# Carrying three dense streams through all stages, and writing a product's bias with one matmul

## The reference

```
h = relu(layernorm(x)); x = x + gcn(h, edges)
h = relu(layernorm(x)); x = x + sage(h, edges)      # two convolutions with W_l, W_r, b
h = relu(layernorm(x)); x = x + mlp_gnn(h, edges)   # messages by a 2-layer MLP, update by one, layernorm, gamma, beta
h = relu(layernorm(x)); x = x + mean_gnn(h, edges)  # W_self, W_neighbor, bias
```

## Time and profile before

| | |
|---|---|
| median of 3 runs | 6238.43 us |
| profiled execution, span | 6243.6 us |
| PE busy | 4227.3 us, 68% |
| DVE busy | 4147.6 us, 66% |
| ACT busy | 3656.1 us, 59% |
| POOL busy (inside DMA instructions) | 3838.7 us, 61% |
| mean granted PE clock | 0.836 |

### The profile page before, as it was taken

One profiled execution on the slowest core, in us unless ns is written; L12 is line 12 of the kernel. 1 busy time (PEld: TensorE's weight loads), 2 busy tenths in 40 slices (PEclk: granted clock), 3 DMA queues, 4 the chain that ended last, 5 costly groups with the idle time before them and its releaser, 6 DMA issues. The chain is left out here.

```text
span 6243.6 us, 88780 instructions
## 1 busy us (share of the span) xinstructions
PE 4227.3 (68%) x25124; PEld 3337.9 (53%) x25124; DVE 4147.6 (66%) x20553; ACT 3656.1 (59%) x9152; POOL 3838.7 (61%) x3228
## 2 busy tenths in 40 slices
PE   1173777777566766998958888886888846545444
PEld 1052555556455555777736666664666634434333
DVE  1094777778699995776747777785999945434334
ACT  0003767767577774776746677774877845434333
POOL 6605666675577765776747677765777654544554
PEclk7596888888788887999979999998999967667666
DMA  9903656666466664666658788884555531211221
GB/s 251 311 2 112 181 154 172 167 166 169 115 153 151 148 144 113 146 144 132 130 147 220 209 225 216 225 204 113 136 132 128 122 77 58 76 53 63 66 65 36
DMA packets 891523, 878.84 MB, mean 141 GB/s; under 512 B 131106, under 2 KB 671660, under 8 KB 890962
## 3 DMA queue, kind: packets, MB, share of 16 engines
q1 hardware_dynamic: 546568, 575.48, 29.0%
q0 software_dynamic: 224000, 235.91, 22.7%
q10 hardware_dynamic: 120460, 61.78, 3.7%
HBM read 345.70 MB, written 533.16 MB: 141 GB/s over the span
## 5 line engine op out<-in xcount | busy, mean ns | idle before, releaser
L2061 POOL DMA_INDIRECT out<-final_y,leads x200 | 202.2, 1011 | 434.8 <-DVE final_y L2188 328.8
L1151 POOL DMA_INDIRECT node<-gcn_comb,leads x200 | 325.2, 1626 | 193.0 <-ACT gcn_comb L1176 92.5
L1151 POOL DMA_INDIRECT sums<-mean_comb,leads x200 | 327.6, 1638 | 154.1 <-ACT mean_comb L1176 84.4
L1151 POOL DMA_INDIRECT node<-sage_comb,leadh x200 | 329.4, 1647 | 142.4 <-DMA node<-sage_comb,leadh 60.8
L444 PE MATMUL final_p<-wT,final_hT 128*128 128x128 f32 x800 | 223.0, 393 | 274.9 <-remote 141.4
L1151 POOL DMA_INDIRECT sums<-mlp_same,leadh x200 | 325.7, 1628 | 131.4 <-issue 54.2
L1151 POOL DMA_INDIRECT node<-sage_comb,leadd x200 | 319.5, 1597 | 140.7 <-issue 54.2
L839 PE MATMUL hist<-lo,hi 128*126 128x400 f16 x800 | 162.1, 361 | 261.4 <-issue 136.3
L444 PEld LDWEIGHTS final_p<-wT,final_hT 128*128 128x128 f32 x800 | 170.8, 264 | 305.1 <-remote 144.9
L569 POOL DMA_INDIRECT mlp_a<-node,gidx x200 | 207.2, 1036 | 197.2 <-DVE mlp_v L1778 128.6
L785 DVE TENSOR_SCALAR hi<-iota,parts 128x252 f16<-128x252 f16 x400 | 146.0, 378 | 245.7 <-remote 159.0
(11 more groups left out here) (367 smaller groups left out, 17207.2 us busy)
## 6 DMA issues: line engine op xcount, KB each, us to landing
node<-b SPq DMA_DIRECT2D x400, 256.0 KB
sums<-zero_row SPq DMA_DIRECT2D x400, 256.0 KB
node<-zero_row ACTq DMA_DIRECT2D x50, 1152.0 KB
sage_dx<-in_x SPq DMA_DIRECT2D x70, 256.0 KB
out<-sage_dy SPq DMA_DIRECT2D x70, 256.0 KB
gcn_dx<-in_x SPq DMA_DIRECT2D x66, 256.0 KB
out<-gcn_dy SPq DMA_DIRECT2D x66, 256.0 KB
x_src<-xs SPq DMA_DIRECT2D x50, 256.0 KB
```

The lines of the kernel that those rows point to most:

```text
L1151: pool.indirect_dma_start(table, bass.IndirectOffsetOnAxis(ap=leads[:, i * G + c, t:t + 1], axis=0), e.comb[c][:, t, :], None, element_off ...
L2061: pool.indirect_dma_start(table, bass.IndirectOffsetOnAxis(ap=idx[:, t:t + 1], axis=0), rows[:, t, :], None, bounds_check=N - 1, oob_is_er ...
```

## The change

- The dense rows are worked on by three streams of 55, 54 and 54 rounds (`PARTS`) that are created once (`gnn_program`), with their own buffers, banks and semaphores, and run on through the five edge stages; in gcn three more streams of 11 rounds (`MORE`) run beside them. 163 + 33 = 196 rounds.
- `Plan` takes, for each stream and step, the rounds already begun. In a stage with carried streams it stops when all the other work is done and the next step would begin over 3 us (`OVERHANG`) after it; what is left of the dense steps goes to the next stage. In mean it runs to their end. Dense streams have a period of their own.
- `mix_u2` of a round in gcn or sage1 adds the residual by PE as before; since a round may cross a seam, every round has a `res` step, which there only counts.
- `rows_matmul` writes the bias first, into all 512 columns, by one matmul; `brow` is four times as wide, filled by four DMAs in setup.
- sage1 uses `whole=True`: one `add` of four DMAs, six match tiles, `combine_columns(..., True)`; its adds use `leadd`.
- sage2 has three banks for three streams; no bank is shared by dense streams.
- Planner costs of products with bias are 150 ns less (mix3 of the last stage 200), and `TIMES` is new for all stages.

```diff
-DENSE = {"gcn": (11,) * 6, "sage1": (10,) * 3, "sage2": (10,) * 4, "mlp": (10,) * 3, "mean": (10,) * 3}
+PARTS = (55, 54, 54)
+MORE = (11, 11, 11)
+ND = len(PARTS)
...
-    "gcn": (232002, (
+    "gcn": (90000, 75000, (
...
-    "sage1": (64400, (
+    "sage1": (66000, 68000, (
...
-    "sage2": (90926, (
+    "sage2": (64500, 45000, (
...
-    "mlp": (122112, (
+    "mlp": (92000, 85000, (
...
-    "mean": (64783, (
+    "mean": (65000, 66000, (
...
-    "final": (1175445, (
+    "final": (77000, 0, (
...
+OVERHANG = 3000
...
-        self.next, self.end, self.deps, self.ready = 0, [], [], None
+        self.next, self.end, self.deps, self.ready = begun, [release] * begun, [], None
...
+            if left == 0 and at > over + OVERHANG:
+                break
             begin, line = min((a for a in able if a[1].node.eng == first.node.eng and a[0] <= at + PATIENCE),
-                              key=lambda a: (a[1].next * period + a[1].when, a[1].s, a[1].j))
+                              key=lambda a: (a[1].next * period[a[1].s] + a[1].when, a[1].s, a[1].j))
...
+def make_plan(streams, phase, dn=None, last=False, more=None):
+    period, every, times = TIMES[phase]
+    begun = [[0] * len(nodes) for nodes in streams]
+    many, periods = [RD] * G, [period] * G
+    if dn is None:
+        return Plan(streams, begun, many, periods, times, ())
+    kept = range(G, G + ND)
+    streams, begun = streams + dn.nodes(phase), begun + dn.begun
+    if more is not None:
+        streams, begun = streams + more.nodes(phase), begun + more.begun
+    many += list(dn.many) + (list(more.many) if more else [])
+    plan = Plan(streams, begun, many, periods + [every] * (len(streams) - G), times, () if last else kept)
+    dn.begun = plan.next[G:G + ND]
+    for d in (dn,) if more is None else (dn, more):
+        d.start_phase(phase, plan, G if d is dn else G + ND)
+    return plan
...
 def rows_matmul(nc, ps, xT, w, plus=None, bias=None):
+    if bias is not None:
+        nc.tensor.matmul(ps[:, :], bias[0], bias[1], start=True, stop=False)
     for t in range(T):
         o = ps[:, t * P:(t + 1) * P]
-        last = nc.tensor.matmul(o, xT[:, t * P:(t + 1) * P], w, start=True, stop=plus is None and bias is None)
+        ends = bias is None or t == T - 1
+        last = nc.tensor.matmul(o, xT[:, t * P:(t + 1) * P], w, start=bias is None, stop=ends and plus is None)
         if plus is not None:
-            last = nc.tensor.matmul(o, plus[0], plus[1](t), start=False, stop=bias is None)
-        if bias is not None:
-            last = nc.tensor.matmul(o, bias[0], bias[1], start=False, stop=True)
+            last = nc.tensor.matmul(o, plus[0], plus[1](t), start=False, stop=ends)
     return last
...
-        self.brow = sb("brow", [P, 5, D], BF16)
+        self.brow = sb("brow", [P, 5, CH], BF16)
...
-            act.dma_start(k.brow[0:3, :, :], tb.split.rearrange("b s f -> s b f")).then_inc(split_in, 16)
-            act.wait_ge(split_in, 32)
+            for t in range(T):
+                act.dma_start(k.brow[0:3, :, t * D:(t + 1) * D], tb.split.rearrange("b s f -> s b f")).then_inc(split_in, 16)
+            act.wait_ge(split_in, 16 + T * 16)
...
+RES = {"gcn": TENSOR, "sage1": TENSOR, "sage2": VECTOR, "mlp": VECTOR, "mean": VECTOR}
...
     if name == "res":
-        dve.wait_ge(dn.stored[d], i * 16 + 1)
         dve.wait_ge(done, at.before(i, name))
-        nc.vector.tensor_tensor(flat(y[:, :, :]), p[:, :], flat(h[:, :, :]), ALU.add).then_inc(done, 1)
+        if dn.on[d, i] == VECTOR:
+            dve.wait_ge(dn.stored[d], i * 16 + 1)
+            nc.vector.tensor_tensor(flat(y[:, :, :]), p[:, :], flat(h[:, :, :]), ALU.add).then_inc(done, 1)
+        else:
+            dve.sem_inc(done, 1)
...
-                 + edge_tail(True, SCALAR) + fill_nodes(FILL))
+                 + edge_tail(True, SCALAR, whole=True) + fill_nodes(FILL))
...
-                    add_pair(pool, e, plan, tb.node, k.leadh, name, i, c, W1)
+                    add_pair(pool, e, plan, tb.node, k.leadd, name, i, c, W1)
...
-                    combine_columns(nc, e.p[c], e.same[c], h[c]).then_inc(e.done[c], 1)
+                    combine_columns(nc, e.p[c], e.same[c], h[c], True).then_inc(e.done[c], 1)
```

More of the change, by code:

```diff
@@ L274, with __init__ @@
 class Plan:
-    def __init__(self, streams, many, period, when):
+    def __init__(self, streams, begun, many, period, when, carried):
         lines = []
@@ L293, in __init__ @@
         every = [line for own in lines for line in own]
+        left, over = sum(line.many for line in every if line.s not in carried), 0
         for line in every:
```

249 lines of the change are left out of this document (117 added, 132 removed), and 350 rows, old and new, of the table TIMES.

## The result

The changed kernel takes 6164.75 us (median of 4 runs, 6158.69 to 6175.01) against 6238.02 us before: ratio 0.9891, 95% interval 0.9864 to 0.9918. It is faster by 73 us where 428 were forecast. The profiled execution has a span of 6159.1 us, 6160.85 with what lies around it.

The account below looks back on a forecast made before the run. No stage sits on an engine's limit; the missing shares lie in seam holes and late results. Setup 486+3, edge stages 4282 (4582 before) and last stage 1045 give 5816, less 5: 5810 us; range 5420 to 6240.

Parts of the forecast that it names:

- gcn and mlp would become denser: Edge stages: fullest engines rise to 82% and 87% in gcn (1040 us), from 81 to 89% in mlp (1030 us).
- The price of the bias: Products: one 512-column bias matmul costs 0.23 us against 0.44 for four, saving 0.21 at full clock, twice that at half.
- What it is worth: Bias saving on the path: 25 and 30 us in sage2 and mlp; hidden in gcn, sage1, mean; 65 us of last-stage PE.
- Whole matching: sage1: two more match tiles a chunk cost DVE 40 us; at most 40 us of landing waits go, mostly not showing.
- Rounds per stage: Dense rounds, read from due-time medians: about 67, 28, 37, 33, 31 against 66, 30, 40, 30, 30; shifts little.
- Seams: Holes of 60 to 75 us between stages: carried streams fill a third of each, 85 us in four.
- Late results: Seams and last stage: finished work whose waiter hears only when POOL pauses; 392 us of the last stage's chain.
- Last stage: New table takes away a third of its 392 us of late results: 1045 us, bounds 820 and 1340.
- little gain: Rival, 20%: stages stay as dense, seams give 85 us, bias 55, last stage 55, DVE adds 47: 6090 us (6000 to 6220).
- As planned: Rival, 15%: the order lets POOL run through, stages 3915 us and last 773+45: 5222 us with setup.
- Slower: Rival, 8% plus 2% for other order losses: last stage's POOL and PE times add to 1342 us, kernel 6420 us.
- The page on SBUF: POOL's DMAs: DVE on the second port pair shuts GpSimd out, lengthening adds; some 30 to 90 us on the path.

Follow-up runs that it names:

- after_again: The changed kernel, same program, run once more in group C1: 5237.6 us, ratio 0.9962 to the kernel before.
- A: Group of runs on one chip, kernel before at 6234 us; held the bias alone (6080.5 us), b_bias_last and p1_probe.
- B2: Group of runs on one chip, kernel before at 6096 us; held the changed kernel (6043), the bias alone (5982) and moved dense rounds (6072).
- b_bias_2: The kernel before with only the bias changed to one 512-column matmul ahead of the products, run in B2: 5982 us, ratio 0.9828.
- bl_again: b_bias_last run once more, beside the changed kernel in C1: 5255.0 us, ratio 0.9995 to the kernel before.
- b_bias_last: The kernel before with the new bias and the changed kernel's last-stage due times and product lengths: 6047.3 us, ratio 0.9712.
- p1_probe: Separate probe, no reference work: counting beside 48 unbroken gathers took the same 60 us as alone; TensorE-ScalarE hand-over 91.9 us against 83.5 alone.
- p2_probe: Separate probe, no reference work: counting beside gathers, stores and fills; gathers alone stretched 89 us of counting to 156, fills with gathers left it at 88.
- C1: Group of runs on one chip, kernel before at 5251 us, nothing late; held after_again, bl_again, the paused setup (5272.2) and a third probe.
- C2: Group repeating the four programs of C1, kernel before at 5257 us, nothing late: ratios 0.9957, 0.998, 1.0029 and the same probe result.
- the pause: b_bias_last with a waited-for 256-column memset behind each setup gather: 5272.2 us, ratio 1.0039 in C1, and 1.0029 in C2.

## Why the prediction was right or wrong

The direction and the range were right, the size was wrong: 5815 us were forecast for the span and 6159 came. By stages the misses are gcn +90, sage1 +4, sage2 +18, mlp +147, mean +4, last +79, setup +1. Two steps of the sum carry 316 of these 343 us. One is that gcn and mlp would become denser ("at 82% and 87%", "from 81 to 89%"): VectorE and GpSimd fill 77 and 80% of gcn, and TensorE 78% of mlp, less than the 81 before. The other is the third of the last stage's late results, 130 us, that was taken away: 372 us stayed of 392. Where nothing is late, in after_again, gcn is at 89% (VectorE) and mlp at 87% (TensorE), so the densities of the sum are reached there, and late results and the five rounds more in mlp are what they left out.

- **The price of the bias** was right: 0.21 and 0.43 us a matmul, forecast 0.23 at full clock. **What it is worth** was wrong in this condition: with late results the bias alone gives 153 us (A) and 114 (B2), where 55 and some for the last stage were counted. Calling it hidden in gcn and mean failed; those gave 58 and 46 us. Without late results 55 was too much: bias and last table together give 0 to 10 us there (ratios 0.9995 and 0.998), although TensorE is busy for 3937 us in b_bias_2 against 4227 before by the pages' sums (across groups). Why shorter products should shorten a stage in which TensorE waits isn't shown.
- **Whole matching**: the mechanism was right, the price too high: 28 us more VectorE where 40 were forecast, sage1 24 us longer, nothing back from landings. That sage1 came out at 784 for a forecast of 780, and mean at 746 for 742, is partly luck: both hold fewer rounds than forecast (24 for 28, 29 for 31), and VectorE fills 87% of each where 92 and 90 were counted on.
- **Rounds per stage**: this step failed too. The median of due times gave 67, 28, 37, 33, 31; the trace has 71, 24, 37, 35, 29. A round more was priced at 9 us of VectorE and 8 of TensorE and taken as beside other work or at par; measured, with late results, five rounds more make mlp 72 to 80 us longer and gcn 66 to 73 in the old frame, 13 to 16 us a round, while six fewer in sage1 give back 7. With that, mlp's 1030 had no ground: the forecast let its density rise from 81 to 89% on the strength of filled seams. The price holds for this condition only: between bl_again and after_again, where nothing is late, mlp's five rounds more come with 18 us and gcn's with 5 less, though there the frame changes too.
- **Seams**: right in kind and half in size. A third of each was to be filled, some 85 us in four; VectorE has 49 us more in them and TensorE 38. The reading that "the other seams look alike" was wrong: VectorE had 25 us of work in the first and 6 in the third. Work put into a seam is also work that late results can hold up: VectorE's wait in the third grew from 31.6 to 35.7 us.
- **Late results**: they were seen rightly and are larger than they were taken for: the kernel is 714 to 816 us shorter without them, of which the prediction had the last stage's part and the seams, and not the 144 to 160 us in the setup or those inside gcn and mlp. That the new tables would take a third of them away was a guess without a row, and failed as a term of the sum: 372 us of the last stage's chain are unknown after, 392 before. Taken apart it is two effects. With the bias alone the unknown part of that chain is 442 us (A) and 449 (B2); with the new table it is 330 in b_bias_last (A), and 323 and 292 in B2. So the table does take 112 to 157 us of it away, but the stage becomes only 27 us shorter in A, as other waits take the place in the chain. "POOL's unbroken rows" as the whole cause failed in p1_probe, and the waiter that "hears of it only when POOL pauses" failed in p2_probe, where it hears in mid-row.
- **Last stage**: 1045 forecast, 1124 measured, 29 us from the bias and 27 from the table; the failing term is the 130 us for late results, of which 20 came.
- **Rivals**: "little gain" (6090, range 6000 to 6220) is what happened, and in its main point for its reason: stages stay as dense as they were. But its terms weren't met singly: the bias is worth 114 to 153 us where it had 55 and a part of the last stage's 55, and the new frame loses 61 where it had a gain from seams less 47 us of VectorE, so that 6165 lies near 6090 partly by luck. "As planned" (5222) is nearly the time of the kernel in C1 (5238), for a reason that has nothing to do with the change. "Slower" in its place, the last stage, didn't come.
- **The page on SBUF**: gathers take 0.94 us by themselves and 1.41 beside VectorE's unbroken f16 tiles in p2_probe. So the rule of the Trainium skill, SBUF - State Buffer, section "SBUF: two separate sides", that VectorE on the second port pair keeps GpSimd out of it, agrees with the trace there, if these tiles use the second port pair, which no trace shows. In the kernel its price stayed small: beside the unbroken f16 tiles of after_again's setup a gather takes 1.02 us, and adds take 1606 to 1633 ns in all edge stages after, none near the 1700 named. In C2, with VectorE at 80% of the span in place of 69 in B2, adds take 1608 to 1640 ns against 1602 to 1631.
- **The signs named**: gcn under 1100 us and 200 to 300 us of unknown releasers in the last stage did not come (1130 and 372); sage1 hardly shorter, and 838 biases of 512 columns, did (838 weight loads at L466, though the matmuls last 0.38 us and not 0.25, with the next one 0.21 us behind).

## What to carry to other kernels

Undo a change in parts before judging it: here one part was worth 153 us and the rest gave most of that back, and the version made of the good parts (`b_bias_last`, ratio 0.9712) has the lowest ratio measured where results are late. A busy table and a sum of engine needs say what a stage could take; a wait on "an unknown releaser" is a term of its own that no engine's saving removes, and it needs a measurement beside the kernel before any forecast counts on it. When work moves between stages, count where it lands in the trace's order, and price a unit by what a stage grew by when it got one. And cut windows at the same point of both kernels: counted from the first gather on, the seams hold 122 us of VectorE before and 131 after, and counted around it 52 and 101.

## What the runs showed of the hardware

The same program on the same chip took 6115 us in one group of runs and 5257 in another, with steady times inside each. What sets the two apart in the traces is results of TensorE that their waiters hear of up to 43 us late, and what follows from it, the lower granted clock among it: the changed kernel is 160 us longer in the setup, 111 in gcn and 308 in the last stage. Late results were there in the four groups whose kernel before took 6096 to 6238 us, and in neither of the two at 5251 and 5257. They come while GpSimd issues indirect DMAs, and in the setup they outlast it: in all ten kernel traces with late results VectorE's last late wait there ends at 313 to 318 us, 24 to 29 us after the start of the last gather, and in the changed kernel no transfer runs from 305 to 315. The waiter can hear in the middle of a row of gathers. VectorE's and ScalarE's messages to each other were not late in the probe.

GpSimd's pace isn't the cause by itself: the setup's gathers start one in 1.28 us with late results and one in 1.31 without, and rows at 1.25 us were harmless in the groups without. Whether the pace matters once the condition is there stays open, as the pause that was to tell it ran only in groups without late results, and so does what sets the condition.

The changed kernel and b_bias_last never ran in one group with late results, so that b_bias_last is the faster there rests on two steps: 61 us between the changed kernel and the bias alone in B2, and 33 between the bias alone and b_bias_last in A.
